# A two-layer perceiver block on one core: streams of short steps by a table, scores in row strips, context mixed by probabilities

## What is computed

```python
x = x + L0_xattn(layernorm(x), ctx)   # 16 heads of 8; query i sees only the 16 keys 16*i to 16*i+15
x = x + L0_attn(layernorm(x))         # RWKV: three mixes with the token before, a running max and two scans over 32 steps
x = x + L0_ffn(layernorm(x))          # 8 experts of 64 (top 2 by sqrt(softplus)) and a shared one, silu
x = x + L1_xattn(layernorm(x), ctx, ctx, mask)  # 16 heads of 8; all 512 keys, masked at the end
x = x + L1_attn(layernorm(x))         # linear attention (relu) with a 128-512-128 feed-forward, gelu
x = x + L1_ffn(layernorm(x))          # 16 experts of 512 with 32 slots each, top 1 by softmax
```

## Time and profile before

| | us |
|---|---|
| median of 3 runs | 320.88 |
| lowest and highest of them | 319.68, 323.71 |
| span of the profiled execution | 314.4 |
| busy: TensorE, VectorE, ScalarE, POOL | 283.4, 213.5, 133.5, 42.9 |

### The profile page before, as it was taken

The page is one execution under the profiler, slowest core; times in us unless marked ns, Lnnn a source line. Parts: engine busy times, 40 slices in busy tenths (PEclk is TensorE's granted clock), DMA queues, the critical chain, the costliest instruction groups (busy, mean ns, idle before and its releaser), DMA issues.

```text
span 314.4 us, 4937 instructions
## 1 busy us (share of the span) xinstructions
PE 283.4 (90%) x1836; PEld 175.7 (56%) x1836; DVE 213.5 (68%) x536; ACT 133.5 (42%) x281; POOL 42.9 (14%) x63
## 2 busy tenths in 40 slices
PE   6998899898889878888979999999997988989996
PEld 5333346343636845445547565556755566777766
DVE  3556865889753559998582856996884676752572
ACT  1204333342541256546952556456439940132120
POOL 4200000000220530212300331121010001010000
PEclk9999999999999999999997999999999999999999
DMA  7999000000000075005000500000000069100001
GB/s 281 454 349 202 6 3 0 0 2 0 1 0 0 0 302 234 0 2 136 0 1 2 134 3 0 2 1 2 0 2 0 2 259 401 44 0 2 0 2 33
DMA packets 3111, 22.52 MB, mean 72 GB/s; under 512 B 400, under 2 KB 1424, under 8 KB 1808
## 3 DMA queue, kind: packets, MB, share of 16 engines
q1 hardware_dynamic: 3088, 22.21, 20.3%
HBM read 21.95 MB, written 0.26 MB: 71 GB/s over the span
## 4 chain that ended last, share of the span: by engine, by line
PE 30%; issue 12%; DVE 10%; ACT 4%; POOL 2%; POOLq 0%; DVEq 0%
PE bank L1275 9%; PE bank L1285 5%; PE bank L1297 3%; PE bank L1427 2%; PE bank L1488 1%; PE bank L1356 1%; PE bank L1348 1%; PE bank L1479 1%; PE bank L1461 1%; ACT work_sb L574 1%; PE bank L1094 1%; POOL rstd_sb L340 1%; DVE work_sb L907 1%; POOL small_sb L408 1%; DVE mask_sb L931 1%
## 5 line engine op out<-in xcount | busy, mean ns | idle before, releaser
L1275 PE MATMUL bank<-k_sb,work_sb 128*128 128x512 f32 x128 | 68.1, 616 | 3.8 <-DVE small_sb L907 2.7
L574 ACT ACTIVATE work_sb<-work_sb,small_sb 128x512 f32<-128x512 f32 x48 | 34.7, 722 | 43.3 <-DVE small_sb L907 43.3
L907 DVE CUSTOM_DVE_ANT_0 work_sb<-bank,mask_sb 128x512 f32<-128x512 f32 x48 | 33.1, 689 | 15.3 <-PE bank L1275 13.9
L1285 PEld LDWEIGHTS bank<-early_sb,work_sb 128*128 128x128 f32 x192 | 23.6, 142 | 30.3 <-issue 19.1
L340 POOL TENSOR_TENSOR rstd_sb<-veps_sb,minus_half_sb 128x2 f32<-128x2 f32 (+1 forms) x13 | 10.1, 774 | 171.9 <-DVE veps_sb L672 152.5
L1285 PE MATMUL bank<-early_sb,work_sb 128*128 128x128 f32 x192 | 29.0, 274 | 3.3 <-ACT work_sb L581 3.1
L1427 PE MATMUL bank<-work_sb 128*128 128x256 f32 x94 | 24.3, 402 | 1.3 <-POOL work_sb L328 1.3
L1275 PEld LDWEIGHTS bank<-k_sb,work_sb 128*128 128x128 f32 x128 | 20.0, 192 | 9.3 <-DVE small_sb L907 4.6
L914 DVE COPY work_sb<-bank 128x512 f32<-128x512 f32 x32 | 21.9, 685 | 0.3 <-PE bank L1285 0.3
L367 POOL TENSOR_TENSOR work_sb<-work_sb,late_sb 128x512 f32<-128x512 f32 x16 | 16.8, 1064 | 38.4 <-PE bank L1275 30.8
L1427 PEld LDWEIGHTS bank<-work_sb 128*128 128x128 f32 x94 | 18.2, 203 | 4.0 <-POOL work_sb L328 1.3
(11 more groups left out here) (233 smaller groups left out, 466.0 us busy)
## 6 DMA issues: line engine op xcount, KB each, us to landing
ctx_sb<-moe_w SPq DMA_DIRECT2D x1, 4096.0 KB, 13.9
k_sb<-moe_w SPq DMA_DIRECT2D x1, 4096.0 KB, 13.7
ctx_sb<-ctx SPq DMA_DIRECT2D x3, 1024.0 KB, 16.3
late_sb<-late SPq DMA_DIRECT2D x1, 2903.0 KB, 14.6
mask_sb<-mask SPq DMA_DIRECT2D x4, 512.0 KB, 24.1
mask_sb<-mask SPq DMA_DIRECT2D x8, 256.0 KB, 4.6
v_sb<-moe_b SPq DMA_DIRECT2D x1, 1280.0 KB, 11.8
ctx_sb<-ctx SPq DMA_DIRECT2D x2, 512.0 KB, 5.7
```

The costliest lines, as they stand in the source:

```text
L574: s.activation(sc[u % NSC], sc[u % NSC], ACT.Exp, bias=smin[:, u:u + 1], scale=-1.0, accum_out=rsum[:, u:u + 1]).then_inc(sig("p1_ready"), 1)
L907: v.tensor_tensor_reduce(sc[u % NSC], bank[u % NS][:, :], mask[:, KEYS * b:KEYS * (b + 1)], MASK_BIG, 3e38, ALU.add, ALU.min, smin[:, u:u ...
L1275: mm(bank[u % NS][:, :], qbd[b % NQ][:, P * g:P * (g + 1)], k1[:, KEYS * b:KEYS * (b + 1)], start=True, stop=True).then_inc(sig("s1_ready" ...
L1285: last = nc.tensor.transpose(bank[2 + u % NT][:, P * k:P * (k + 1)], sc[u % NSC][:, P * k:P * (k + 1)], wt("ident"))
```

## The change

**The order.** Each engine's work is now cut into streams, generators that yield after nearly every instruction, or every few matmuls: L (local attention), P (projections), a and b (`small_stages` of half 0 and 1), S (scores, on DVE minima, on ScalarE exponentials), T (turns, on ScalarE copies), V (outputs, on DVE `take_heads`), c (`linear_stages(0)`), d (`linear_stages(1)` and the experts), F and G (matmuls of 128 columns that nobody reads). `TURNS` gives for each engine the order in which steps are taken: `L10` is ten steps of L. Semaphores of the two halves are separate now (`x0_new`, `x1_new` and so on). DVE's `ch.link` is split into `add`, a yield, and `join`, so that steps of other streams stand between an instruction and the wait for it. Seven b steps of TensorE and 38 of DVE come before the first score; behind the last turn or minimum come c's steps from 12 on of TensorE and its last 28 of 55 on DVE.

```diff
+TURNS = {
+    "PE": (
+        "L P2 L P L10 P L P4 L P L8 P L2 a L2 P L3 a L2 a3 L P L P7 L P2 L a L6 a L a2 L a b P3 b F P2 b P b "
+        "P2 a P a2 P a3 P F2 b F8 a2 b F3 b S b T b T S2 T3 S V b T b T2 b T2 b3 T2 S V T b T V b T2 S T2 V "
+        "T2 S T2 V T2 S T2 V T2 S T2 V T S T2 c T V T2 S T2 c V T2 S T2 V T c T S c T2 V T2 c T S V T2 c S T2 "
+        "c T V T c T2 c T2 S V T c T2 V T2 c V c d G c d G4 c G d G d2 G3 d3 c d c d G3 d c G8 d G2 d2 G3 d4 "
+        "G5 d G3 d2 G5 d G5 d19 "),
+    "DVE": (
+        "L19 a L a L a L5 a2 L a L a L a L2 a4 L2 a6 L a L a2 L a L a2 L a P a3 L a L3 a L a b a b a L2 a L P "
...
+        def run(engine, **streams):
+
+            for turn in TURNS[engine].split():
+                for _ in range(int(turn[1:] or 1)):
+                    next(streams[turn[0]], None)
+            for name in "LPabSTVcd":
+                for _ in streams.get(name, ()):
+                    pass
+
```

```diff
+        qc = [work[:, P * b:P * (b + 1)] for b in range(BATCH)]
+        QC_HEAD = 2
+        SB, TB, OB1 = (0, 1, 2, 5), (3, 4), 6
+        NSC, NPT = 8, 8
         q1T = tile(15)
-        sc = [tile(4 + i) for i in range(NSC - 1)] + [spare[:, :]]
+        sc = [tile(i, of=ctx) for i in range(NSC)]
...
+        BY_DVE = ()
...
+            def scores():
+
+                for b in range(BATCH):
+                    if b == 0:
+                        pe.wait_ge(sig("o0_ready"), 2)
+                    else:
+                        pe.wait_ge(sig("s1_min"), GROUPS * b)
+                    if b % HB == 0:
+                        for i in (2 * b + len(PROJ) // 2 - 2, 2 * b + len(PROJ) // 2 - 1):
+                            name, n = taker(i)
+                            pe.wait_ge(sig(name), n)
+                    if b % HB in (0, QC_HEAD):
+                        pe.wait_ge(sig("qc_ready"), 2 * (b // HB) + (1 if b % HB < QC_HEAD else 2))
                     for g in range(GROUPS):
...
+                        mm(bank[SB[g]][:, :], qc[b][r, :], k1[r, KEYS * b:KEYS * (b + 1)], start=True, stop=True)\
+                            .then_inc(sig("s1_ready"), 1)
+                    yield
...
+            def turns():
+
+                for u in range(2 * UNITS):
+                    pe.wait_ge(sig("p1_ready"), u + 1)
+                    if u < 2:
+                        name, n = taker(len(PROJ) - 2 + u)
+                    else:
+                        name, n = copied(u - 2)
+                    pe.wait_ge(sig(name), n)
+                    for k in range(KT):
+                        last = nc.tensor.transpose(bank[TB[u % 2]][:, P * k:P * (k + 1)], sc[u % NSC][:, P * k:P * (k + 1)], wt("ident"))
+                    last.then_inc(sig("pT_ps"), 1)
+                    yield
```

```diff
+        def widen(eng, c):
+
+            out = mix[c % NE].rearrange("p (k h q) -> p k h q", k=KT, h=HEADS)
+            probs = bank[2][:, :].rearrange("p (k i n h) -> p k i n h", k=KT, i=4, n=2)[:, :, c % 4, c % HB // 4, :]
+            own = wt("own8").unsqueeze(1).unsqueeze(1).broadcast_to([P, KT, HEADS, TILE_Q])
+            return eng.tensor_tensor(out, probs.unsqueeze(3).broadcast_to([P, KT, HEADS, TILE_Q]), own, ALU.mult)
...
+                    pe.wait_ge(sig("p0_ready"), h + 1)
+                    for k in range(KT):
+                        last = nc.tensor.transpose(bank[2][:, P * k:P * (k + 1)], e0[:, P * k:P * (k + 1)], wt("ident"))
+                    last.then_inc(sig("p0T_ps"), 1)
+                    yield
+                    for c in range(HB * h, HB * (h + 1)):
+                        if c % HB < 2:
+                            pe.wait_ge(sig("prod_ready"), HB * (h + 1))
+                        else:
+                            pe.wait_ge(sig("z_out"), c - 1)
+                        if c % HB == 0:
+                            pe.wait_ge(sig(f"ctok_in{h}"), 16)
+                        pe.wait_ge(sig("mix_in"), c + 1)
+                        for k in range(KT):
+                            at = KEYS * (c % HB) + P * k
+                            last = mm(bank[c % 2][:, P * k:P * (k + 1)], ctok[h][:, at:at + P], mix[c % NE][:, P * k:P * (k + 1)],
+                                      start=True, stop=True)
+                        last.then_inc(sig("z_ps"), 1)
+                        yield
+                    pe.wait_ge(sig("z_out"), HB * (h + 1))
+                    pe.wait_ge(sig("next_in"), 16)
+                    for j in range(4):
+                        for n in range(4):
+                            head = 4 * n + j
+                            last = mm(bank[2][32 * n:32 * n + 32, 0:HTOK], wt("wv0")[:, 32 * head:32 * head + 32], zh[:, head, :],
+                                      start=(j == 0), stop=(j == 3), skip_group_check=True)
+                    last.then_inc(sig("o0_ps"), 1)
+                    yield
 
```

```diff
+            context(0)
+            context(1)
+            context(2)
+            sp.dma_start(following[:, :], next_d).then_inc(sig("next_in"), 16)
+            sp.dma_start(ctok[0], ctok_d[:, 0:CTX // 2]).then_inc(sig("ctok_in0"), 16)
+            context(3)
+            sp.dma_start(late[:, :], late_d).then_inc(sig("late_in"), 16)
+            context(4)
+            sp.dma_start(ctok[1], ctok_d[:, CTX // 2:CTX]).then_inc(sig("ctok_in1"), 16)
+
+            sp.wait_ge(sig("z_ps"), HB)
...
+            sp.wait_ge(sig("pT_ps"), 2 * UNITS)
+            sp.dma_start(ctx[:, :], w1_d).then_inc(sig("w1_in"), 16)
```

```diff
+                    if h and n != 1:
+                        pe.wait_ge(sig("ffh_ready"), (6, 6, 7, 8)[n])
+                    for t in range(HT):
+                        last = mm((B if h else A)[:, P * t:P * (t + 1)], hT[:, HTOK * n + P * t:HTOK * n + P * (t + 1)],
+                                  wt("w2")[:, P * n:P * (n + 1)], start=(n == 0 and t == 0), stop=(n == 3), skip_group_check=True)
+                    if h and n % 2 and n < 3:
+                        yield
```

```diff
+                ch.add(v.tensor_tensor(ge(mr[4]), ge(mr[0]), wide(one(0)), ALU.not_equal))
+                yield
+                ch.join()
+                ch.add(v.scalar_tensor_tensor(ge(mr[4]), ge(mr[4]), float(E1), flat("iota_e"), ALU.mult, ALU.add))
+                yield
+                ch.join()
+                ch.add(v.tensor_reduce(one(4), ge(mr[4]), AX_X, ALU.min))
+                yield
+                ch.join()
+                v.tensor_tensor(ge(mr[5]), flat("iota_e"), wide(one(4)), ALU.is_equal).then_inc(sig("onehot_ready"), 1)
+                yield
                 v.tensor_tensor(ge(mr[1]), ge(mr[0]), wide(one(0)), ALU.subtract).then_inc(sig("gate_arg"), 1)
```

1633 lines of the change are left out of this document (816 added, 817 removed), and 7 rows, old and new, of the table TURNS.

## The result

The changed kernel takes 258.69 us, the median of four runs (256.57 to 260.72), against 321.0 us for the kernel before on the same chip (four runs, 319.68 to 323.71). The ratio is 0.805, with a 95% interval from 0.798 to 0.811: 19.5% less time, where 17% was forecast. The profiled execution of after took 256.57 us, with a span of 254.5 us.

A forecast was written before the change was run, and what follows sets the result against it. TensorE was taken to bound the kernel up to the end of layer 1's attention, and a chain of steps the rest; 107 + 97 + 55 = 259 us of span plus about 6.5 gave 265 us, range about 248 to 298.

The forecast's parts named there:

- about 6.5 lie around it, and they stay: Time around the profiled span: median 320.88 us against span 314.4 before, so about 6.5 us added to the forecast.
- the first part: From 10.7 us to layer 1's first scores: TensorE's 91.5 us of work at 95% packing, 96 us, ending at 107.
- the last part: Half 1's linear stages and the experts, after the attention: 55 us in place of 56.4, between 51 and 60.
- Scores in strips: Layer 1's attention: a batch's four score matmuls run together in 0.86 us, not 3.44; batch 4.0 us instead of 6.40.
- the alternative weighed at 0.26 us per change: Layer 1's attention: each change of shape costs 0.26 us instead of 0.10; batch 4.3 us, stage 5 us more.
- The loads of the stage: Layer 1's attention stage: TensorE 87 us, ScalarE 85, VectorE 68; at 90% busy 97 us in place of 146.
- the transfer of late: ctx_tok's 4 MB moves late's landing from 17 to about 25 us; costed at nothing, some 10 us at half rate.
- The one-hot from the logits: In the last part: no exponential between the maximum and the one-hot; five of ten steps go, 1.4 us.
- the other two terms of that part: In the last part: second feed-forward matmuls follow each Gelu, 1.5 us less; linear stages 0 on DVE, 2 us more.
- Strips in series: Rival in layer 1's attention: score strips run one after another, stage 141 us instead of 97, kernel 309 us; chance 0.09.
- Streams that wait for each other: Rival: engines in fixed orders wait for each other, 75% busy, attention stage 116 us, kernel 292 us; chance 0.18.
- The clock: Rival: TensorE's clock stays low through layer 1's attention, its 87 us of work double, kernel 352 us; chance 0.05.

The follow-up runs named there:

- strips alone: The kernel before, with each of its 64 score matmuls contracting over its own 32 rows only, in the old order of units; 358.91 us.
- strips off: The changed kernel, with each score matmul contracting over all 128 rows instead of its own strip of 32; 289.26 us, ratio to before 0.909.
- copies on VectorE: The changed kernel, with 16 of the 64 copies of turned probabilities moved from ScalarE to VectorE; 268.60 us, ratio to before 0.836.
- full rows: The changed kernel, with the twelve 8-row matmuls of the routing weights widened by 120 rows of zeros; 257.33 us.

## Why the prediction was right, and where it was off

**The sum.** Forecast was 107 + 97 + 55 = 259 us of span; it is 104.3 + 95.5 + 54.7 = 254.5. Each term lies inside its bounds. The forecast of 265 us is 6 us over the median of 258.7.

**The term that was mis-sized most** is the smallest: "about 6.5 lie around it, and they stay". I took the median of three runs (320.88) less the span of one profiled execution (314.4). After has 2.1 us around its span (256.57 less 254.5), and in 25 later runs of before, whose spans and times are told together, 1.7 to 3.6 us lie around them. So some 4 of the 6.5 us weren't around the span at all: the span was of an execution with a high clock (0.995), and later runs of before with that clock took 315.8 to 317.9 us, well under the median of 320.88. A span and a time have to come from the same execution.

Three slips in the sums changed little. The terms of the first part add up to 91.3 us of work, not 91.5; its lower bound at 98% is 104 us, not 103; and the low end of the range takes 49 us for the last part, whose own lower bound was 51.

**Scores in strips.** Of the bounds 0.86 and 3.44 us I took 0.86, since the strips should run as the column strips did. They do: 1.08 us to the next start for four, of which 0.2 were allowed for the two changes of shape. The batch takes 4.13 instead of the forecast 4.0, since the turns on both sides are also longer (two in 1.02 us where 0.88 was usual). So a change of shape seems to cost its neighbour as well, 0.14 us for the two turns on each side; in the kernel with strips alone a single turn between two strips took 0.58 (214.30 to 214.88) where 0.44 was usual. The Trainium skill (TensorEngine Tiling (Array Packing), Key Properties) says that a change drains the array; the alternative weighed at 0.26 us per change would have made the batch 4.3 us. The run shows 4.13, between the two. "What would show it" had 5 to 6 us from outputs to outputs; that is the mean over the stage (fifteen distances from 122.1 to 198.8 us, 5.1 each), and 4.13 is the pace when nothing waits.

**The loads of the stage.** TensorE 87 forecast, 87.2 measured; ScalarE 85 and 87.5; VectorE 68 and 67.5; 90% full forecast, 91% measured. TensorE's 87.2 has some 4 us in it that are due to the low clock (0.96 of 95.5), so its work was 83, and the forecast was right partly because two errors met: the other streams weigh less than the 23 us that I gave them. The step to 90% was a choice, and strips off shows what it depends on: with one bound engine the same order reaches 97%.

**The first part.** Forecast 91.5 us of work at 95% packing, measured 89.0 in 93.2, which is 95.5%. The doubled z matmuls confirm the reading: what is added to TensorE there comes out at the end in full. That the transfer of late costs nothing held too, but narrowly. It was issued at 5.4 us and landed 20.7 us after its issue, at about 26, and the first v projection ran at 26.93 us, without a wait in front:

```profile
26.43 0.66 PE L1258 MATMUL bank<-early_sb,work_sb 128*128 128x128 f32 x4
26.93 1.06 PE L1214 MATMUL bank<-late_sb,ctx_sb 128*128 128x128 f32 x8
27.96 2.29 PE L1271 MATMUL bank<-work_sb,mask_sb 128*128 128x128 f32 x18
```

**The last part.** 55 forecast, 54.7 measured, with no single term of it tested but the filling. The one-hot from the logits stands as expected, on VectorE's timeline of after (compare, where the exponential lay between):

```profile
233.32 0.19 DVE L1079 TENSOR_REDUCE small_sb<-small_sb 128x2 f32<-128x32 f32 x1
...
234.22 0.19 DVE L1091 TENSOR_TENSOR small_sb<-late_sb,small_sb 128x32 f32<-128x32 f32 x1
```

0.9 us from maximum to one-hot instead of 2.25: 1.35 of the 1.4 forecast. No run splits the other two terms of that part. What holds it together is the filling (4 to 5 us, by the run without it).

**The rivals.** Strips in series would have given 309 us; strips off, which is that rival built, took 289. It was over-priced by 20 us, again from a utilisation of 91% that should have been 97%, and from streams that weighed less. Streams that wait for each other: not so in this kernel, since the waits of the minima for TensorE are 12.2 us in all, less than the 13.9 that three of four buffers alone had before, but copies on VectorE shows that the danger is real: 16 moved steps cost some 5 us of waiting, and 5 to 9 us in time. The clock: it does fall, but for 12 us of the profiled execution, worth 5 us (254.5 x 0.02), and not in the middle of the strips, where the rival had it. In the later profiled execution of the same kernel it is worth 12 us (259.2 x 0.046). The forecast's own sum had no term for this, so that its 259 us of span agrees partly because TensorE's loads were taken too high. The rows that I had for it were the better clue: the low clock stood behind matmuls of 8 and 64 rows, and the run with full rows shows that those of 8 matter.

ScalarE: Activation LUTs (What ACT_TABLE_LOAD costs) in the Trainium skill has a drain of about 1.4 us on top of each load. After shows none, as before did: the load at 110.71 us takes 1.28, and the next operation starts at 112.00.

## What to carry to other kernels

Split an expected gain into the bound engine's work and the share of time that it can be busy, and give the second its own number: about 91% with two level engines, 97% with one, in this kernel. Row strips paid side by side, all rows of the array filled, and lost alone. Steps with few rows or a chain with little for TensorE cost twice in this kernel, once as time and once as clock behind them, so mix them with full work, widen them with zero rows where the columns are the same, and fill the gaps that remain.

## What the runs showed of the hardware that was not expected

Four 32-row strips of 512 columns in fp32 delay the next matmul by 1.08 us; one such strip between full matmuls delays it by 1.06. Three of the four are free. The Trainium skill (TensorE: Matmul & The Clock Gate, Measured speedup vs the span model) has 3.07 times for four row strips of 32 rows and 512 columns, and names no type for that row; here, in fp32, it is 4 x 0.86 / 1.08 = 3.2, the changes of shape included.

With the same instructions, columns and order, filling 32 instead of 128 rows in 64 of the matmuls took the mean granted clock from between 0.979 and 0.995 to between 0.842 and 0.925 (TensorE 93% busy), and it fell to 0.50 at 251 us behind 31 us without a gap. Filling 128 instead of 8 rows in 12 matmuls (24 instructions) kept a stretch at 1.00 that had 0.58 (and 0.50 in other runs). In both pairs the changes of the array's shape differ together with the rows. Gaps do it too: 1.14 us of work in 4 us were followed by 0.50, and with the gap filled the clock stayed at 1.00. But in the kernel before TensorE stood still from 157 to 159 us, and the clock stayed at 1.00. The Trainium skill (TensorE: Matmul & The Clock Gate, What's actually happening) ties the clock to how busy TensorE has been. For the filled gap these traces agree; with lone strips in the order, an engine without a gap lost its clock all the same.

How long the clock stays low isn't settled by the kernel alone: the changed kernel's own ten runs have means from 0.954 to 0.980, and its two profiled ones are low for some 4 and for some 14 us ahead of the stage. What decides between them stays open.

VectorE's normalization step (L659, 20 times) takes 380 ns in the changed kernel; in the one before, where GpSimd was busy 42.9 instead of 28.0 us, it took 530. Whether GpSimd is the cause wasn't tried.
